# Attention loop: key splitting, moments and the row of maxima move from VectorE to GpSimd and ScalarE, and the row's transpose stands one unit later

## The reference

```python
def L0_attn(x):                       # the only layer that the change touches
    q, k, v = split(x @ W_attn + b_attn)                 # 16 heads of 16 channels
    q, k = rope(q), rope(k)                              # angles go by head, not by position
    att = einsum('bhqd,bhkd->bhqk', q, k) / sqrt(16)
    att = softmax(where(causal, att, -inf))
    return einsum('bhqk,bhkd->bhqd', att, v) @ W_proj + b_proj
x = x + layernorm(L0_attn(layernorm(x)))
x = x + layernorm(L0_ffn(layernorm(x)))   # top 128 tokens of a batch through attention and a gated FFN
x = x + layernorm(L1_attn(layernorm(x)))  # attention for the 35 queries chosen in each head
x = x + layernorm(L1_ffn(layernorm(x)))   # FFN with dequantised weights
```

## Time and profile before

| | |
|---|---|
| median of 3 runs | 3547.5 us (3546.36 to 3552.07) |
| profiled execution | 3569.1 us, span 3567.4 us |
| busy over the span | PE 2933.1, DVE 2072.3, ACT 1260.0, POOL 545.8 us |
| before the attention loop's first exponential | 116 us |
| its eight turns | 116.1 to 1525.3 us |
| what follows (tail of the last batch, the other three layers) | 1525.3 to 3567.4 us |
| mean granted TensorE clock | 0.907 |

### The profile page before, as it was taken

One profiled execution on the slowest core, in us unless ns is written; L12 is line 12 of the kernel. 1 busy time (PEld: TensorE's weight loads), 2 busy tenths in 40 slices (PEclk: granted clock), 3 DMA queues, 4 the chain that ended last, 5 costly groups with the idle time before them and its releaser, 6 DMA issues. The chain is left out here.

```text
span 3567.4 us, 44916 instructions
## 1 busy us (share of the span) xinstructions
PE 2933.1 (82%) x15561; PEld 1781.8 (50%) x15561; DVE 2072.3 (58%) x5935; ACT 1260.0 (35%) x2085; POOL 545.8 (15%) x701
## 2 busy tenths in 40 slices
PE   3899898989898989943788886489998989999876
PEld 1334343434344444322667775455665656566554
DVE  3777777767676867755466655444525344353442
ACT  1455555555455555631221221013132231313211
POOL 3000202020202020110111211001202012020211
PEclk8899899999999999976888897789999999999998
DMA  4141414132332423131222221200101011010000
GB/s 132 51 126 44 149 43 136 56 112 80 100 92 78 115 72 108 32 110 49 90 89 84 92 97 60 90 12 27 51 0 50 12 38 50 0 50 6 18 24 12
DMA packets 172172, 235.43 MB, mean 66 GB/s; under 512 B 17117, under 2 KB 138873, under 8 KB 165762
## 3 DMA queue, kind: packets, MB, share of 16 engines
q1 hardware_dynamic: 172002, 233.27, 21.3%
HBM read 131.74 MB, written 101.50 MB: 65 GB/s over the span
## 5 line engine op out<-in xcount | busy, mean ns | idle before, releaser
L939 ACT ACTIVATE pt<-ps 128x1024 f32<-128x1024 f32 (+3 forms) x768 | 601.7, 812 | 478.8 <-PE ps L854 331.5
L739 DVE CUSTOM_DVE_ANT_0 masked<-ps,mask_q 128x128 bf16<-128x128 f32 (+3 forms) x1024 | 473.1, 484 | 157.2 <-PE ps L832 152.3
L832 PE MATMUL ps<-sk,sq 96*128 96x512 bf16 (+3 forms) x1536 | 453.2, 349 | 122.2 <-DVE mx L743 47.4
L851 PE MATMUL ps<-sq,sk 99*128 99x512 bf16 (+3 forms) x1536 | 421.9, 343 | 17.4 <-DMA sq<-scratch_nm_parts 13.4
L743 DVE TENSOR_REDUCE mx<-ps 128x1 f32<-128x512 f32 x512 | 350.7, 685 | 97.1 <-PE ps L832 96.5
L832 PEld LDWEIGHTS ps<-sk,sq 96*128 96x128 bf16 x1536 | 138.7, 99 | 472.1 <-issue 147.1
L870 PE MATMUL ps<-pt,val 128*32 128x512 f32 (+3 forms) x3072 | 342.8, 520 | 0.7 <-ACT yt L947 0.6
L1940 PE MATMUL ps<-eht,w_fc 128*128 128x512 f32 x512 | 252.5, 641 | 9.4 <-ACT eht L1991 9.4
L1952 PE MATMUL ps<-w_fc,eyb 128*128 128x256 f32 x1024 | 228.7, 381 | 15.1 <-ACT eyb L1999 15.1
L851 PEld LDWEIGHTS ps<-sq,sk 99*128 99x128 bf16 x1536 | 153.5, 101 | 162.0 <-issue 43.0
L1952 PEld LDWEIGHTS ps<-w_fc,eyb 128*128 128x128 f32 x1024 | 193.2, 190 | 53.3 <-ACT eyb L1999 24.1
(11 more groups left out here) (288 smaller groups left out, 4828.1 us busy)
## 6 DMA issues: line engine op xcount, KB each, us to landing
scratch_stacks<-part SPq DMA_DIRECT2D x32, 768.0 KB, 3.6
sq<-scratch_stacks SPq DMA_DIRECT2D x32, 768.0 KB, 8.0
sk<-scratch_stacks SPq DMA_DIRECT2D x32, 768.0 KB, 9.4
scratch_stacks<-part SPq DMA_DIRECT2D x32, 512.0 KB, 4.5
x<-in_L_attn_x SPq DMA_DIRECT2D x8, 1024.0 KB, 13.6
scratch_stacks<-part SPq DMA_DIRECT2D x32, 256.0 KB, 4.9
xr<-in_L_attn_x SPq DMA_DIRECT2D x8, 1024.0 KB, 6.1
scratch_x<-xr SPq DMA_DIRECT2D x8, 1024.0 KB, 10.2
```

The costliest lines, as they stand in the source:

```text
L739: nc.vector.tensor_tensor_reduce(mem["masked"][:, slot, 0:n], ps[:, RING[slot], 0:n], mem["mask_q"][:, BANK - n:BANK], 1.0, -3e38, ALU.add ...
L832: nc.tensor.matmul(ps[:, bank, 0:n], sq[0:ROWS, h, i * P:(i + 1) * P], sk[0:ROWS, h, half * BANK:half * BANK + n], start=True, stop=True)\
L851: last = nc.tensor.matmul(ps[:, bank, 0:n], sk[0:ROWS_M, h, j * P:(j + 1) * P], sq[0:ROWS_M, h, q0:q0 + n], start=True, stop=not diag)
L939: nc.scalar.activation(pt[:, u % 3, 2 * pair:2 * pair + 2, 0:n], ps[:, bank:bank + 2, 0:n], ACT.Exp, scale=SCALE).then_inc(e["exp_done"], 1)
```

## The change

Key halves are split on GpSimd like query halves. `bn_aggr` is gone from this loop: VectorE does `bn_stats` alone, and GpSimd combines the two half moments that it leaves for each tile, in ten steps for the eight tiles instead of four. The step `rows` is cut in two: `nmax` (the reduction on VectorE) stays at unit 8 of each twelve, the transpose and what follows stand at unit 9. The transposed row is copied from PSUM by ScalarE and split by GpSimd. Since every engine goes through the list in order, this adds places in the order of GpSimd and ScalarE.

Core of the diff:

```diff
-                put(at + 8, ("rows", b, s), ("nm", b, s))
+                put(at + 8, ("nmax", b, s))
+                put(at + 9, ("rows", b, s), ("nm", b, s))
...
-def rstd_and_shift(nc, moments, rstd, shift, w, tmp, ready, count):
-
-
-    nc.gpsimd.tensor_scalar(tmp, moments[:, :, 1], EPS_LN, None, ALU.add).then_inc(ready, 1)
-    nc.gpsimd.tensor_scalar(shift, moments[:, :, 0], -1.0, None, ALU.mult).then_inc(ready, 1)
-    nc.gpsimd.wait_ge(ready, count + 2)
-    nc.gpsimd.tensor_tensor(rstd, tmp, w["mhalf"][:, 0:NT], ALU.pow).then_inc(ready, 1)
-    nc.gpsimd.wait_ge(ready, count + 3)
-    return nc.gpsimd.tensor_tensor(shift, shift, rstd, ALU.mult)
+MOMENT_STEPS = 9
+
+
+def rstd_and_shift(nc, stats, rstd, shift, w, mom, ready, count):
+
+
+    diff, sums, spread_, square = (mom[:, n, :] for n in range(4))
+    g = nc.gpsimd
+    g.tensor_tensor(diff, stats[:, :, 1], stats[:, :, 4], ALU.subtract).then_inc(ready, 1)
+    g.tensor_tensor(sums, stats[:, :, 1], stats[:, :, 4], ALU.add).then_inc(ready, 1)
+    g.tensor_tensor(spread_, stats[:, :, 2], stats[:, :, 5], ALU.add).then_inc(ready, 1)
+    g.wait_ge(ready, count + 1)
+    g.tensor_tensor(square, diff, diff, ALU.mult).then_inc(ready, 1)
+    g.wait_ge(ready, count + 3)
+    g.tensor_scalar(spread_, spread_, 1.0 / C, EPS_LN, ALU.mult, ALU.add).then_inc(ready, 1)
+    g.wait_ge(ready, count + 4)
+    g.tensor_scalar(square, square, 0.25, None, ALU.mult).then_inc(ready, 1)
+    g.tensor_scalar(shift, sums, -0.5, None, ALU.mult).then_inc(ready, 1)
+    g.wait_ge(ready, count + 7)
+    g.tensor_tensor(square, square, spread_, ALU.add).then_inc(ready, 1)
+    g.wait_ge(ready, count + 8)
+    g.tensor_tensor(rstd, square, w["mhalf"][:, 0:NT], ALU.pow).then_inc(ready, 1)
+    g.wait_ge(ready, count + 9)
+    return g.tensor_tensor(shift, shift, rstd, ALU.mult)
...
-                if kind == "parts" and a[0] == 0:
+                if kind == "parts":
                     r, chunk, n = a
                     half = slice(n * BANK, (n + 1) * BANK)
                     until_taken(g, ("qk", b, r, chunk, n))
-                    done = halves_before(b, *a)
+                    done = nth[step]
...
+                elif kind == "rows":
+                    done = nth[step]
+                    until_taken(g, step)
+                    if done:
+                        g.wait_ge(e["nm_out"], 16 * done)
+                    nc.gpsimd.tensor_copy(nmp[:, 0, :], nmr[:, :]).then_inc(e["nm_step"], 1)
+                    g.wait_ge(e["nm_step"], 3 * done + 1)
+                    nc.gpsimd.tensor_tensor(nmr[:, :], nmr[:, :], nmp[:, 0, :], ALU.subtract)\
+                        .then_inc(e["nm_step"], 1)
+                    g.wait_ge(e["nm_step"], 3 * done + 2)
+                    nc.gpsimd.tensor_copy(nmp[:, 1, :], nmr[:, :]).then_inc(e["nm_step"], 1)
+                    g.wait_ge(e["nm_step"], 3 * done + 3)
+                    nc.gpsimd.tensor_tensor(nmp[:, 2, :], nmr[:, :], nmp[:, 1, :], ALU.subtract)\
+                        .then_inc(e["nmp_ready"], 1)
...
-                elif kind == "rows":
+                elif kind == "nmax":
+                    if nth[step]:
+                        until_filled(v, ("rows", *divmod(nth[step] - 1, SETS)))
                     nc.vector.drain()
                     nc.vector.tensor_reduce(nm[:, :, :], mx[:, :, :, :], AX.X, ALU.max, negate=True)\
                         .then_inc(e["nm_ready"], 1)
-                    v.wait_ge(filled[slot], uses + 1)
-                    if nth[step]:
-                        v.wait_ge(e["nm_out"], 16 * nth[step])
-                    nc.vector.tensor_copy(nmr[:, :], ps[0:R, RING[slot], 0:P]).then_inc(taken[slot], 1)
-                    nc.vector.drain()
-                    nc.vector.tensor_copy(nmp[:, 0, :], nmr[:, :])
-                    nc.vector.drain()
-                    nc.vector.tensor_tensor(nmr[:, :], nmr[:, :], nmp[:, 0, :], ALU.subtract)
-                    nc.vector.drain()
-                    nc.vector.tensor_copy(nmp[:, 1, :], nmr[:, :])
-                    nc.vector.drain()
-                    nc.vector.tensor_tensor(nmp[:, 2, :], nmr[:, :], nmp[:, 1, :], ALU.subtract)\
-                        .then_inc(e["nmp_ready"], 1)
-                elif kind == "parts" and a[0] == 1:
-                    r, chunk, n = a
-                    half = slice(n * BANK, (n + 1) * BANK)
-                    until_taken(v, ("qk", b, r, chunk, n))
-                    if chunk:
-                        v.wait_ge(e["parts_out"][r], 16 * len(RUNS[r]) * (b + 1))
-                    elif b:
-                        v.wait_ge(e["parts_out"][2 * (KC - 1) + r], 16 * len(RUNS[r]) * b)
-                    nc.vector.tensor_copy(part[:, r, 0, half], qk[:, r, half])
-                    nc.vector.drain()
-                    nc.vector.tensor_tensor(qk[:, r, half], qk[:, r, half], part[:, r, 0, half], ALU.subtract)
-                    nc.vector.drain()
-                    nc.vector.tensor_copy(part[:, r, 1, half], qk[:, r, half])
-                    nc.vector.drain()
-                    nc.vector.tensor_tensor(part[:, r, 2, half], qk[:, r, half], part[:, r, 1, half], ALU.subtract)\
-                        .then_inc(e["parts_ready"][r], 1)
                 elif kind == "x_stat":
...
-                    last = layer_stats(nc, mem["tstats"], mem["tmv"], att[:, i, :], i)
+                    last = nc.vector.bn_stats(mem["tstats"][:, i, :], att[:, i, :])
...
+                elif kind == "rows":
+                    act.wait_ge(filled[slot], uses + 1)
+                    if nth[step]:
+                        act.wait_ge(e["nmp_ready"], nth[step])
+                    nc.scalar.copy(nmr[:, :], ps[0:R, RING[slot], 0:P]).then_inc(taken[slot], 1)
```

More of the change, by code:

```diff
@@ L515, in attention_steps @@
     order += [("stack", 0, s) for s in range(SETS - 1)] + [("v", 0, 0, n) for n in range(NHALF)]
-    order += [("max", 0, 0, n) for n in range(len(MU))] + [("rows", 0, 0), ("nm", 0, 0)]
+    order += [("max", 0, 0, n) for n in range(len(MU))] + [("nmax", 0, 0), ("rows", 0, 0), ("nm", 0, 0)]
     order += [("max", 0, 1, n) for n in range(EARLY)]
@@ L781, in _ @@
                         v.wait_ge(e["x_in"], 16 * b)
-                    last = layer_stats(nc, mem["hstats"], mem["hmv"], x[:, j, :], j)
+                    last = nc.vector.bn_stats(mem["hstats"][:, j, :], x[:, j, :])
                     if j == NT - 1:
@@ L807, in _ @@
                     v.wait_ge(e["x1_ready"], NT * b + j + 1)
-                    last = layer_stats(nc, mem["tstats"], mem["tmv"], xr[:, j, :], j)
+                    last = nc.vector.bn_stats(mem["tstats"][:, j, :], xr[:, j, :])
                     if j == NT - 1:
```

22 lines of the change are left out of this document (11 added, 11 removed).

## The result

| | before | after | ratio [95%] |
|---|---|---|---|
| median of 4 runs | 3547.9 us (3546.4 to 3552.1) | 3528.5 us (3520.2 to 3528.9) | 0.9941 [0.9926, 0.9956] |
| same kernels in a later session (after 6 runs, before 12) | 3555.9 us (3525.3 to 3564.1) | 3527.7 us (3515.9 to 3533.5) | 0.9914 [0.9893, 0.9935] |
| profiled execution, span | 3569.1, 3567.4 us | 3520.2, 3518.2 us | |
| the eight turns in it | 1409.2 us | 1373.2 us | |

So the change gains 19 to 28 us. The two profiled executions lie 49 apart, which is too much: before's was 21 above its own median, and what follows the loop, whose matmuls are the same 6910, took 13.9 us less in after's (TensorE busy 1613.8 and 1595.2 us there, granted clock 0.88 and 0.89). The turns account for the other 36. Within a turn most differences repeat from turn to turn, and I read the cause from these.

What follows compares the result with a forecast made beforehand. TensorE was taken to set the pace, losing about 20 us a turn to waits. Gains of 87 less 83.5 given back left 3.5 us, so 3547.5 becomes 3544; 8 in 10 within 3508 to 3582, own range 3530 to 3560.

Steps and rivals of the forecast that it cites:

- The likeliest case: Whole kernel: old waits go, new ones behind GpSimd's work nearly cancel the gain; 3544 us, chance 0.40.
- rival 1: New waits come back shorter (splits 1.1 us) and the clock does not fall after them: 3516 us, chance 0.25.
- place A: Unit 9: row's steps, then moments, delay ScalarE's copy that frees TensorE's bank; 5.0 us plus 2.4 for clock, loss 50.
- place B: Unit 21: row waits behind GpSimd's key half and adds, delaying unit 24; 1.4 of 5.9 us stay, gain 14.
- place C: Unit 34: tail's moments behind unit 33's row delay normalisation and unit 36; 3.2 us in 6 turns, loss 22.
- place D: Unit 45: row to exponentials takes 7.3 us against 6.8 for three units; 0.5 in 7 turns, loss 3.5.
- the row's 8: Units 20, 32, 44: transpose one unit later spares TensorE's wait for the row, 0.3 to 0.5 each, gain 8.
- The gains: Relief from VectorE's work: 30 at units 29 and 30, 28 at 5 to 8, 8 at 20, 32, 44, 7 at 13 to 17.
- The ends: Outside the loop: 4 for key halves ahead, 5 with first moments and row; 3 behind for moments in the open.
- Rival 2: GpSimd becomes the bound: slower small steps lengthen 20 waits, deciding from splits of about 2.3 us; 3576 us, chance 0.25.
- Rival 3: Relief falls beside work TensorE does anyway, so only half the claimed relief is real: 3581 us, chance 0.10.

Runs made afterwards that it cites:

- fix_abc: Changed kernel with input moments at unit 8, tail moments at unit 27 and first chunk's key halves at units 22 and 23: 3428.8 us, 0.9653 of before.
- slow_splits: Changed kernel with the last subtraction of each row's split done four times, each waiting for the one before: 3580.6 us, 1.0060 of before.

## Why the prediction was right, and where not

The forecast was 3544, the time 3528.5. The likeliest case (waits replaced by other waits, in the places named) is what happened, and the wide range of 3508 to 3582 holds the time. The forecast's own range of 3530 to 3560 does not, by 1.5 us, and rival 1's 3516 is somewhat nearer than 3544. The sign was partly luck: it had 0.42 against 0.40, and hung on 3.5 us left between 87 and 83.5, where place A alone was 17 us off. The median gained 19 us where the sum had 3.5; between the profiled executions it is 49, of which the turns make 36.

Some sums do not come out as they are written. In place B the steps give 744.9 and the row 748.5, not 745.1 and 748.9, and 1.4 us in six turns and 4.5 in the first make 12.9, not 14. In place C 11.8 less 8.9 is 2.9, not 3.2; in place D the terms make 7.15, not 7.3. Put right, they would make the sum some 5 us larger.

Its terms against the profile, over the eight turns (differences of the groups of the table, with the first and last turn from their own rows):

| units | term | predicted | measured |
|---|---|---|---|
| 0 to 8 | combinations, row, transpose | +28 | +24 |
| 13 to 19 | a combination less per tile | +7 | +8 |
| 20 to 28 | key halves against the later row (B), row at 20 | +14 and +3 | +12 |
| 29 to 32 | key halves, row at 32 | +30 and +3 | +37 |
| 37 to 44 | row at 44 | +3 | +11 |
| 9 to 12 | A | -50 | -33 |
| 33 to 36 | C | -22 | -19 |
| 45 to 47 | D | -3.5 | -3.3 |
| sum of the turns (the row's 8 is spread over three groups as 3 each) | | +11.5 | +36 |
| ahead of the loop, behind it | | -5, -3 | -1, 0 |

**Place A failed in size**, by 17 of the 25 us that the turns differ. The step was "5.0 us, and 2.4 for the clock after it". TensorE indeed stands from 5.7 us after the unit's start (670.85 - 3.56 = 667.29, unit 9 at 661.62), but its release came at 9.2 and not at 10.7. Of these 1.5 us, the row's copy being done earlier (first split at 1.93, predicted 2.35) and splits of 1.6 instead of 1.8 make 0.65, and the moments 0.6: 3.8 us (665.14 to 668.93) instead of 4.4. I had charged each of the six new steps 0.20 to 0.25 with 0.08 to the next. Those that wait for nothing start 0.17 apart (665.14, 665.31). And the low clock cost 1.7 us, not 2.4: in units 10 and 11 TensorE is busy 8.37 us in after and 6.65 in fix_abc (means of the six middle turns). These make 2.0 of the 2.7 us a turn by which the term was off; most of the rest is time that units 9, 11 and 12 lost before the change and that the term did not count (10.3 us before, 9.8 in fix_abc).

**Place B was right in its chain and wrong in its worth.** The row was to come in 13.8 us after unit 21's start (748.9 against 735.10); unit 24 starts 13.8 after it (730.28 - 716.46). But the clock term was left out there. The clock falls at 726.4, inside the wait of 5.00 us (725.28 to 730.28), and stays at 0.50 until 736.7. Unit 24 takes 8.74 us (mean of the six middle turns) against 7.58 before, where part of it ran at 0.50 as well (748.6 to 755.4), and 6.49 in fix_abc. Against before that is 1.2 us a turn or 7 us, of which units 20 to 23 gave 2 back; the term came out 5 us too high.

**Place C was right in its sum, by two misses that cancel.** The shift was predicted at 8.0 and came at 7.0, the exponential's release at 9.75 and came at 8.7, unit 36 at 11.8 and came at 11.83, because the clock, for which the term had nothing, was low from 774.2 on and slow matmuls filled the difference. The transfer took the 1.5 us predicted for it.

**The gains were right but for what the clock adds.** Units 37 to 44 gained 11 instead of 3. About half of that is unit 37 (0.7 us a turn). Before, the granted clock was 0.50 from 799.8 to 806.6, in units 36 and 37; now it is low from 774.2 to 781.0, in units 35 and 36, with place C. That is a shift from one term to another that I did not make. The rest is unit 44, where the transpose one unit later gave 0.7 us a turn, as it did at unit 32 (0.6 at unit 20), not 0.3 to 0.5.

**The ends.** All eight halves on one engine were to cost 5 us ahead of the loop; the first exponential came at 116.8 instead of 116.1. GpSimd started on the first half at 44.04, 2.6 us earlier than before, and was done at 73.7, not 76.2. Why it started earlier no run here isolates.

**Rival 1** (waits shorter, no fall of the clock; 3516) got half of it: at units 10 and 35 TensorE was released 1.5 and 1.0 us sooner than computed, but the clock fell at all three places. **Rival 2** (GpSimd as the bound) needed splits over 2.3 us; they took 1.6. slow_splits shows that its mechanism is real and its slope steeper than I wrote: 53 us for 1.5 us, or 18 instead of 10 for each half microsecond, since place D joins and slow matmuls add to it. By that slope splits of 2.3 us would have added 25 us to the time of after and left it level with before, so the threshold was about right. **Rival 3** (relief beside TensorE's work) is refuted: the waits on VectorE fell from 46.5 to 8.8 us, and units 0 to 8 and 29 to 32 gave what was claimed.

What the prediction did not ask is what the change would be worth without the three places. It computed them as prices of the change, as if they came with the work on GpSimd; fix_abc shows that they came with the order, and that 93 to 102 us, several times the measured gain, were in three places of the list.

The Trainium skill (GPSIMD Engine Reference, section on performance versus the Vector engine) gives GpSimd some 2.6 cycles an element for two inputs; at 1.2 GHz I estimate 0.26 us for the 120 columns between a step of 8 and one of 128. The trace has 0.22 (0.20 and 0.42), so it agrees in size. The same page's warning on shared SBUF interfaces (Key points) was the reason I gave rival 2 its chance, and it did not decide here: in after the adds of place B take 0.71 each (713.50, 1.42 for two, and 1.41 for the others), not 0.95 as the four in the earlier trace rows, beside which VectorE split key halves.

## What to carry to other kernels

Before work goes to a nearly idle engine that issues in order, ask for each wait of the critical engine what stands ahead of its releaser in that engine's list; GpSimd was busy 27% of a turn and still cost TensorE three waits of 3.5 to 5 us. When parts of a change gain 109 us alone and 19 to 28 together, look for the places where they queue behind each other, not for a smaller change. And a short chain between two engines may be best left where it was: taking the row from a VectorE that was no longer the bound brought nothing.
